# A triangle-attention stage: v2 refilled bank by bank in PSUM, x in four buffers, sums ahead of the turns, copies in runs of four

## The reference, cut to what matters

```python
q = (x_in @ Wq).reshape(B, N, N, H, d_k)      # B 2, N 64, H 8, d_k 32
k = (x_in @ Wk).reshape(B, N, N, H, d_k)      # v1, v2 likewise
scores = jnp.einsum('bilhd,bljhd->biljh', q, k) / np.sqrt(d_k)
att = jax.nn.softmax(scores, axis=2)          # over l
out = jnp.einsum('biljh,bilhd,bljhd->bijhd', att, v1, v2)
attn_out = out.reshape(B, N, N, E) @ Wo
```

## Time and profile before

| | |
|---|---|
| median of 3 runs | 2622.8 us (2618.41 to 2623.33) |
| profiled execution | 2627.98 us, span 2626.2 us |
| busy shares of the span | PE 82%, DVE 79%, ACT 51%, POOL 42% |
| mean granted TensorE clock | 0.951 |
| start and end of the product loop | 326.4 and 1264.7 us |
| chunk boundaries in it | 450.0, 570.1, 693.4, 812.2, 932.1, 1050.7, 1157.8 us |

### The profile page before, as it was taken

How to read it: one execution, slowest core, us unless ns; L and a number is a source line. 1 busy time by engine, 2 the same in 40 slices (tenths; PEclk the granted TensorE clock), 3 DMA queues, 4 the chain that set the end, 5 groups by cost and what they waited for, 6 DMA issues and landing times. The chain is left out here.

```text
span 2626.2 us, 42406 instructions
## 1 busy us (share of the span) xinstructions
PE 2162.6 (82%) x16632; PEld 1397.0 (53%) x16632; DVE 2087.7 (79%) x2361; ACT 1332.6 (51%) x2690; POOL 1098.6 (42%) x513
## 2 busy tenths in 40 slices
PE   8885686768567767556599997899999999999998
PEld 7764531113122212111277775777777777777776
DVE  4323389999899999999477775788888888888886
ACT  3344457656675776444223233555555555545553
POOL 1101288998899899999211000111112111111111
PEclk9988889889898989899899998999999999999999
DMA  6756223112312111110222322432223223333332
GB/s 216 230 177 186 100 59 66 27 32 50 72 19 44 32 33 19 34 26 12 83 90 91 97 73 65 81 77 74 67 65 78 72 79 92 81 87 91 93 85 57
DMA packets 302502, 204.43 MB, mean 78 GB/s; under 512 B 202720, under 2 KB 280032, under 8 KB 297696
## 3 DMA queue, kind: packets, MB, share of 16 engines
q1 hardware_dynamic: 293600, 168.17, 26.5%
q0 software_dynamic: 8704, 33.56, 3.5%
HBM read 133.76 MB, written 67.90 MB: 77 GB/s over the span
## 5 line engine op out<-in xcount | busy, mean ns | idle before, releaser
L494 PE MATMUL att_bank<-att_av,att_w 128*32 128x512 f32 x4096 | 553.2, 640 | 308.0 <-DVE att_av L339 265.1
L339 DVE TENSOR_TENSOR att_av<-att_att,att_v2ps 128x2816 f32<-128x2816 f32 x240 | 725.7, 3076 | 52.6 <-PE att_bank L494 52.6
L339 POOL TENSOR_TENSOR att_av<-att_att,att_v2sb 128x1280 f32<-128x1280 f32 x240 | 716.9, 3003 | 62.9 <-PE att_bank L494 59.2
L494 PEld LDWEIGHTS att_bank<-att_av,att_w 128*32 128x32 f32 x4096 | 128.9, 113 | 654.2 <-issue 356.5
L630 ACT ACTIVATE att_ev<-att_bank 128x512 f32<-128x512 f32 x512 | 295.6, 598 | 354.2 <-PE att_bank L494 279.9
L1665 DVE SCALAR_TENSOR_TENSOR mb_cv<-mb_bank,mb_cw,mb_cv 128x504 f32<-128x504 f32 (+2 forms) x480 | 343.1, 730 | 126.7 <-ACT mb_cv L1488 121.8
L1308 POOL TENSOR_TENSOR mb_rstd<-mb_ms,mb_neghalf 128x4 f32<-128x4 f32 x32 | 32.2, 1008 | 793.8 <-DVE mb_ms L1709 793.8
L1369 PE MATMUL mb_bank<-mb_xT_hi,dt_win_hi 128*128 128x512 f32 x576 | 242.2, 420 | 36.8 <-DVE mb_cv L1665 35.4
L1427 PE MATMUL mb_bank<-mb_wf,mb_y 128*128 128x256 f32 x1024 | 245.2, 387 | 0.8 <-DVE mb_y L1705 0.8
L1369 PE MATMUL mb_bank<-mb_xT_lo,dt_win_hi 128*128 128x512 f32 x576 | 229.2, 398 | 0.0
L1369 PE MATMUL mb_bank<-mb_xT_hi,dt_win_lo 128*128 128x512 f32 x576 | 228.9, 397 | 0.0
(11 more groups left out here) (184 smaller groups left out, 3675.7 us busy)
## 6 DMA issues: line engine op xcount, KB each, us to landing
att_xin<-in_x SPq DMA_DIRECT2D x32, 512.0 KB, 4.4
qk_t<-att_qk POOLq DMA_DIRECT2D x16, 1024.0 KB, 5.0
v<-att_vs POOLq DMA_DIRECT2D x16, 1024.0 KB, 5.2
mixed_t<-att_ev SPq DMA_DIRECT2D x1024, 8.0 KB
mb_dAb<-dA_rows SPq DMA_DIRECT2D x32, 512.0 KB, 5.8
mb_dAb<-dA_cols SPq DMA_DIRECT2D x32, 512.0 KB, 6.3
att_q<-qk_t SPq DMA_DIRECT2D x8, 1024.0 KB, 9.9
att_kb<-qk_t SPq DMA_DIRECT2D x128, 64.0 KB, 2.1
```

The lines of the kernel that those rows point to most:

```text
L339: eng.tensor_tensor(av[t % 2][:, :, d0:d1, :], a.unsqueeze(2).broadcast_to((P, 2, d1 - d0, N)), v2.unsqueeze(1).broadcast_to((P, 2, d1 - d ...
L494: mm = pe.matmul(bank[r % NB][s * M:(s + 1) * M, :], w[i // WB % 2][:, i % WB, s, :], av[r // 2 % 2][:, i % 2, s * STRIP_D:(s + 1) * STRIP ...
```

## The change

1. `v2in` is no longer an operand of a product (`FRESH` is gone). v2 for GpSimd gets two buffers, filled at step 27 of the chunk before. For VectorE the last and the first product of each chunk are cut in three pieces, one a PSUM bank; as soon as the old chunk's piece has read its bank, ScalarE fills it with the new v2 (between its evictions), and the new chunk's piece waits for that bank only.
2. `xin` has four buffers, and `load_x` runs that much further ahead in SP's order.
3. In the value stage `invert(0, k)` stands before VectorE's evictions of a chunk instead of behind them.
4. `copy_scores` and `copy_att` go over their elements in another order: four neighbours in SBUF in a row, read from PSUM 128 elements apart.
5. The 16 groups of scores take 11 steps, one and two in turn, the exponentials begin at step 13 instead of 18, and the loads of k parts stand two, two, one and one ahead of the first four stores. v2 of the next chunk is loaded without waiting for the first two products.

```diff
-    FRESH = 2
+    NX = 4
@@
-            xin = [e_.sb(f"xin{u}", [P, TT, E]) for u in range(2)]
+            xin = [e_.sb(f"xin{u}", [P, TT, E]) for u in range(NX)]
-        v2sb = sb("v2sb", [P, DK - DD, N])
+        v2sb = [sb(f"v2sb{u}", [P, DK - DD, N]) for u in range(2)]
@@
-        PER_STEP = [0] * 18 + [2] * 12 + [1, 0, 1] + [2, 2, 1] * 8
+        GROUPS_PER_STEP = [1, 2] * 5 + [1] + [0] * 53
+        GROUPS = [range(sum(GROUPS_PER_STEP[:m]), sum(GROUPS_PER_STEP[:m + 1])) for m in range(STEPS)]
+        PER_STEP = [0] * 13 + [2, 1] * 7 + [1, 1, 1, 0, 0, 1] + [2, 2, 1] * 10
@@ load_x
-                    need(sp, transposed, 2 * u - 2)
+                    need(sp, transposed, 2 * (u - NX) + 2)
@@ SP's order before the loop
-            for u in range(2, XN + 2):
+            for u in range(2, XN + 4):
                 load_x(u)
...
             load_q(0)
             load_k(0, 0)
             load_k(0, 1)
-            load_x(XN + 2)
-            load_x(XN + 3)
+            for v in (4, 5, 6):
+                load_x(XN + v)
             load_k(0, 2)
-            load_x(XN + 4)
+            load_x(XN + 7)
...
             load_k(0, 7)
-            load_x(XN + 7)
+            load_x(XN + 10)
             load_q(1)
             load_k(1, 0)
             load_k(1, 1)
-            for v in range(8, 11):
+            for v in range(11, 15):
                 load_x(XN + v)
...
@@ SP's order in the loop
                 if c + 1 < NC:
-                    sp.wait_ge(v2_in_ps, c + 1)
-                    sp.wait_ge(av_by_dve, c * (N // 2) + FRESH)
-                    sp.wait_ge(av_by_pool, c * (N // 2) + FRESH)
+                    sp.wait_ge(v2_in_sb, c + 1)
+                    sp.wait_ge(v2_in_ps, 3 * c + 3)
                     load_v2(c + 1)
                 for e in range(N // EB):
-                    if c % 2 == 0 and n < PAIRS and e < N // KL - 2:
-                        load_k(n, e + 2)
+                    if c % 2 == 0 and n < PAIRS:
+                        for k in {0: (2, 3), 1: (4, 5), 2: (6,), 3: (7,)}.get(e, ()):
+                            load_k(n, k)
                     store(c, e)
@@ VectorE, value stage
             for v in range(XN):
+                if v in SUM_BESIDE:
+                    invert(0, SUM_BESIDE[v])
                 evict_v(v, 1)
...
-                if v in SUM_BESIDE:
-                    invert(0, SUM_BESIDE[v])
@@ VectorE, loop
-                product(dve, t, v2_in_ps, av_by_dve, v2d, 0, DD)
+                wait_for_att(dve, t)
+                need(dve, i_done, 2 * t - 2)
+                if first or last:
+                    for i, (lo, hi) in enumerate(PIECES):
+                        if first:
+                            dve.wait_ge(v2_in_ps, NP * c + i + 1)
+                        ins = product(dve, t, v2d[:, lo:hi], lo, hi)
+                        if last and i + 1 < NP:
+                            ins.then_inc(v2_read, 1)
+                    ins.then_inc(av_by_dve, 1)
+                else:
+                    product(dve, t, v2d, 0, DD).then_inc(av_by_dve, 1)
@@ ScalarE
-                act.activation(raw[:, :, :, g * LB:(g + 1) * LB].rearrange("p j h l -> p l h j"),
-                               X_[g % 2][:, :].rearrange("p (l h j) -> p l h j", l=LB, h=2), ACT.Copy, scale=-SCALE)\
+                act.activation(raw[:, :, :, g * LB:(g + 1) * LB],
+                               X_[g % 2][:, :].rearrange("p (l h j) -> p j h l", l=LB, h=2), ACT.Copy, scale=-SCALE)\
@@
-                act.activation(att[n % 2][:, :, g * JB:(g + 1) * JB].rearrange("p m j -> p j m"),
-                               X_[g % 2][:, :].rearrange("p (j m) -> p j m", j=JB), ACT.Copy).then_inc(t_copied, 1)
+                act.activation(att[n % 2][:, :, g * JB:(g + 1) * JB],
+                               X_[g % 2][:, :].rearrange("p (j m) -> p m j", j=JB), ACT.Copy).then_inc(t_copied, 1)
+            def turn_v2_of_pool(c):
+                act.wait_ge(v2_loaded, c * 32 + 32)
+                need(act, av_by_pool, (c - 1) * (N // 2))
+                act.activation(v2sb[c % 2][:, :, :], v2raw[:, DD:], ACT.Copy).then_inc(v2_in_sb, 1)
+            def turn_v2(c, i):
+                if c == 0:
+                    act.wait_ge(xT_lo_ready, 4 * XN)
+                elif i + 1 < NP:
+                    act.wait_ge(v2_read, (NP - 1) * (c - 1) + i + 1)
+                else:
+                    act.wait_ge(av_by_dve, c * (N // 2))
+                lo, hi = PIECES[i]
+                act.activation(v2d[:, lo:hi], v2raw[:, lo:hi], ACT.Copy).then_inc(v2_in_ps, 1)
...
+                evict(c, 2 * step)
+                if c + 1 < NC and step == N // 2 - 2:
+                    turn_v2(c + 1, 0)
+                evict(c, 2 * step + 1)
+                if c + 1 < NC and step == N // 2 - 5:
+                    turn_v2_of_pool(c + 1)
+                if c + 1 < NC and step == N // 2 - 2:
+                    turn_v2(c + 1, 1)
+                    turn_v2(c + 1, 2)
+                if n < PAIRS:
+                    for g in GROUPS[m]:
+                        copy_scores(n, g)
```

More of the change, by code:

```diff
@@ L177, in block_attention @@
         qk_w_loaded, v_w_loaded, w_split = sem("qk_w_loaded"), sem("v_w_loaded"), sem("w_split")
-        x_loaded = [sem(f"x_loaded{u}") for u in range(2)]
+        x_loaded = [sem(f"x_loaded{u}") for u in range(NX)]
         transposed, xT_hi_ready, xT_lo_ready = sem("transposed"), sem("xT_hi_ready"), sem("xT_lo_ready")
@@ L296, in _ @@
                 load_v1(0, half)
-            for v in range(11, XN):
-                load_x(XN + v)
+            load_x(XN + 15)
             for u in range(2):
@@ L320, in _, with product, wait_for_att @@
                 sp.wait_ge(o_stored[u], 16 * STRIP_D * (B * PAIRS * N // EB // 2))
-        def product(eng, t, v2_ready, ready, v2, d0, d1):
-            pr, c, m = t // STEPS, t // (N // 2), t % (N // 2)
+        PIECES = [(lo, min(lo + BANK // N, DD)) for lo in range(0, DD, BANK // N)]
+        NP = len(PIECES)
+        def product(eng, t, v2, d0, d1):
+            a = att[t // STEPS % 2][:, t % STEPS * 2:t % STEPS * 2 + 2, :]
+            return eng.tensor_tensor(av[t % 2][:, :, d0:d1, :], a.unsqueeze(2).broadcast_to((P, 2, d1 - d0, N)),
+                                     v2.unsqueeze(1).broadcast_to((P, 2, d1 - d0, N)), ALU.mult)
+        def wait_for_att(eng, t):
             if t == 0:
@@ L329, in product @@
             if t % STEPS == 0:
[L330 to L340, removed]
+                eng.wait_ge(t_copied, att_copied(t // STEPS))
         @block.gpsimd
@@ L367, in _ @@
                 n, m = t // STEPS + 1, t % STEPS
-                product(pool, t, v2_in_sb, av_by_pool, v2sb[:, :, :], DD, DK)
+                c = t // (N // 2)
+                wait_for_att(pool, t)
+                if t % (N // 2) == 0:
+                    pool.wait_ge(v2_in_sb, c + 1)
+                need(pool, i_done, 2 * t - 2)
+                product(pool, t, v2sb[c % 2][:, :, :], DD, DK).then_inc(av_by_pool, 1)
                 if n < PAIRS and m in NORM_AT:
@@ L389, in copy_att @@
                 dve.wait_ge(turned, n * (N // JB) + g + 1)
-                dve.tensor_copy(att[n % 2][:, :, g * JB:(g + 1) * JB].rearrange("p m j -> p j m"),
-                                X_[g % 2][:, :].rearrange("p (j m) -> p j m", j=JB)).then_inc(t_by_dve, 1)
+                dve.tensor_copy(att[n % 2][:, :, g * JB:(g + 1) * JB],
+                                X_[g % 2][:, :].rearrange("p (j m) -> p m j", j=JB)).then_inc(t_by_dve, 1)
             def split_w(n):
@@ L439, in _ @@
                     copy_att(0, 2 * TURN_BESIDE[v] + 1)
-                if v in SUM_BESIDE:
-                    invert(0, SUM_BESIDE[v])
             for t in range(PAIRS * STEPS):
                 n, m = t // STEPS + 1, t % STEPS
-                product(dve, t, v2_in_ps, av_by_dve, v2d, 0, DD)
+                c, first, last = t // (N // 2), t % (N // 2) == 0, t % (N // 2) == N // 2 - 1
+                wait_for_att(dve, t)
[10 more added lines that the diff above has]
+                    product(dve, t, v2d, 0, DD).then_inc(av_by_dve, 1)
                 if n < PAIRS and m in LEAST_AT:
@@ L499, in turn_x @@
                 if u < 2 * XN:
-                    pe.wait_ge(x_loaded[u % 2], u // 2 * 16 + 16)
+                    pe.wait_ge(x_loaded[u % NX], u // NX * 16 + 16)
                     if u == XN:
@@ L508, in turn_x @@
                             mm = pe.transpose(T_[u // XN][k][:, tile * P:(tile + 1) * P],
-                                              xin[u % 2][:, tile, k * P:(k + 1) * P], ident[:, :])
+                                              xin[u % NX][:, tile, k * P:(k + 1) * P], ident[:, :])
                         mm.then_inc(transposed, 1)
@@ L561, in _ @@
                     row(t // (N // 2), t % (N // 2) * 2 + i)
-                if n < PAIRS and m < NG:
-                    scores(n, m)
+                if n < PAIRS:
+                    for g in GROUPS[m]:
```

(18 more changed lines are left out.)

16 lines of the change are left out of this document (4 added, 12 removed).

## The result

The changed kernel takes 2496.46 us (median; 2493.52 to 2502.54), against 2623.07 for the kernel before: a ratio of 0.9524, interval 0.9501 to 0.9546. That is 126.6 us less. The forecast was 141 less; the measured time lies 14 us above it and inside its range. Measured again beside three of the experiments, the same kernel gave 0.953.

The account below looks back on a forecast made before the run. It took VectorE to bound the product loop and a chain of waits the value stage. Savings of 78 (loop), 24 (x) and 39 (inverses) make 141, from 2627.98 to 2487 profiled, 2482 as median; range 2440 to 2535.

Parts of the forecast that it names:

- The refill: Product loop, chunk boundaries: 72.2 us from slow products and 20.0 from waits saved, 3 and 4 lost to pieces: 85.
- The waits for banks: Product loop, chunk boundaries: split pieces wait 0 to 1 us a boundary for their refilled bank, 0 to 8, taken as 4.
- Scores in 11 steps, k two at a time: Heads of pairs in the product loop: SP's crowded stores and loads delay VectorE, 7 us lost for three heads (0 to 15).
- x in four buffers: Before and in the value stage: both TensorE waits for x shrink, with clock and first norm wait: 24 us saved (18 to 28).
- the second crowd: TensorE's second x wait, 10.38 us, by the next pair's loads: evictions still wait for a v store; 6.5 saved (3 to 10).
- Sums and inverses: Value stage: GpSimd's norm is done before the turns need it, 103.6 us become 65: 39 saved (31 to 43).
- Copies: Copies of scores and att: no change in time, 0 to 3 us, for any copy length from 0.60 to 1.6 us.
- (c): Copies of scores and att: strided PSUM reads cost double, 2.2 us each, 66 us more, 2548; chance 0.07.
- (d): Same copies: at 2.9 us each the change gains nothing, above that it is slower; chance 0.03 slower, 0.01 level.
- Rival (a): Product loop: stores and loads take the bound in the heads, loop gains 45 instead of 78, 2515; chance 0.18.
- its sign (over 12 us of idle in a head): Heads of pairs: VectorE idle above 12 us in a head would show stores and loads as the bound.
- Rival (b): Value stage stays a chain of waits at low clock, 45 saved there instead of 63, 2500; chance 0.12.

Follow-up runs that it names:

- v2_late: The changed kernel with v2's load for the next chunk behind a chunk's seventh store instead of ahead of the first: 2499.52 us, 0.954 of the kernel before.
- head_old: The changed kernel with the refill kept but the old pace of scores, exponentials and k loads in the heads: 2479.11 us, 0.9462 of the kernel before.
- slow_products_back: The changed kernel with only the refill undone, so the first two products of each chunk read v2in again: 2574.71 us, 0.9824 of the kernel before.
- k_by_act: The changed kernel with k parts 2 to 7 of a pair issued by ScalarE's queue instead of SP's: 2470.64 us, 0.9428 of the kernel before.

## Why the prediction was right, and where it was off

*The refill* (85, as 72 + 20 - 3 - 4): 78 by the undone part, 80.9 in the loop's trace. The mechanism held: the slow products and the eight waits behind them are gone. The pieces cost what was taken: three pieces and one product are 6.2 us at 260.47 of the timeline, so 3.2 for a split product. The waits for banks, taken as 4 in all, are 1.1 us. By these prices the refill would be worth 88; 78 to 81 came, and some 4 of the difference is idle time in the heads that the slow pairs had hidden (41.3 us with the refill, 37 without it).

*Scores in 11 steps, k two at a time* (7 lost, 0 to 15): this is the term that was mis-sized. In the kernel with slow products it costs 13.3 (951.6 against 938.3), with the refill 17 to 18. Its sign was right, its size was not: 17 to 18 lies above the range given for it. Two things went wrong. First, of a loss of 7 to 10 us that I gave to a head, most was to be in the old kernel already; its heads had 19.6 us in three, the new ones 41.3, so 22 came in (some 17 with the new pace, some 5 with the refill, by the two runs that undo one of them). Second, I had followed the stores to ScalarE, lag by lag, and found their lateness of about 13 us; but TensorE also waits for k part 2 itself, because the store of the old rows and v2's load stand ahead of it, and behind this wait the clock is 0.50. That wait is the smaller part (v2_late). With 17 in place of 7 the forecast would be 2492.

*x in four buffers* (24, 18 to 28): 19.9 ahead of the first turn, the place that the 24 were given for. First scores at 135.11 for 134.3; the wait behind the second crowd is 4.82, where about 4 was reckoned. That undoing it costs 25, nearly the forecast 24, is luck: those 25 hold a third wait, and added alone to the old kernel it gains 17.

*Sums and inverses* (39, 31 to 43): the mechanism held, no turn waits for GpSimd, but the size is above the range. The stretch of 103.6 us, forecast at 65 (60 to 72), takes 57.6: 46.0 less. The bound of 60 was 71.6 x 0.84, the busy time at the mean clock of the stretch; at a clock of 1.00 TensorE is busy 56.0 us in it. So the 63 for the stage, measured 65.9, is a sum in which x came 4 lower and the inverses 7 higher. Undone singly, the two cost 24.7 + 48.9 = 73.6 at the start of the loop, and added singly they gain 17.0 + 41.2 = 58.2. The prediction had them add up; they don't, and at least the third wait for x of 10.02 us is a cost that only the one without the other has.

*Copies* (0 to 3 for anything up to 1.6 us each): 0, with the copies at the lower bound. Rivals (c) and (d), dear PSUM reads in steps, did not come: 0.60 us for 512 elements each 512 bytes from the next. So what the Trainium skill (SBUF — State Buffer, "Door 1: The DMA port swizzle") says of 16-byte lines agrees with the writes here, 1.11 scattered and 0.60 in runs of four. Of PSUM's lines of 8 bytes it says that a non-contiguous pattern slows matmuls; the prediction carried that over to the copies, and in their reads by ScalarE or VectorE no such cost is seen. The runs don't separate runs of two from runs of four.

Rival (a), stores and loads as the bound, held in part: it named the right mechanism, its sign (over 12 us of idle in a head) came, and 10 of its 33 us (67.6 for 78 in the loop). Rival (b) is out: TensorE is busy 56.0 of 57.6 us.

## What to carry to other kernels

When a stall goes, ask which queue had lived on it, and count apart what the same change puts on that queue. VectorE's idle time in the three heads, beside the waits behind slow products, was 19.6 us in the kernel before, 24.4 with the refill and the old pace (head_old), 37 with the new pace and no refill (slow_products_back) and 41.3 with both. So the slow pairs had hidden some 5 us of SP's lag, and the new pace cost some 17. Moving v2's load within the queue gained nothing (v2_late), fewer loads ahead of each store gained with the old pace 17 (head_old), a second queue 26 (k_by_act), and both 34.

And a wait of TensorE costs more than its length when the granted clock is lower behind it: in one chunk 4.54 us of waiting cost 6.35, and eight waits of 32.3 us in all cost 48.9. That is 1.4 and 1.5 times, here and for this work.

Two changes that remove waits in one stage need not add up: price each with the other in place as well.

## What the runs showed that was not expected

Four DMA issues of a k part took 2.1 to 2.8 us on ScalarE's queue and 1.83 on SP's, and ScalarE stood still meanwhile (up to 2.26 us before an eviction). It was still worth it, by 26 us. The reads of PSUM in steps of 512 bytes were as fast as reads in a row, for ScalarE (0.60 us) and VectorE (0.68).
